# Splitting the dequantised weights on ScalarE and GpSimd instead of GpSimd alone, with another order of TensorE's small steps, in a fused attention and LoRA kernel

## The reference

```python
x + attention(xn) + ffn(xn)
# attention: q, k, v = xn @ ((qw - 8) * repeat(scales, 128)); 32 query heads and 8 key/value heads of 128,
#            rope on q and k, scores / sqrt(128), causal softmax, values, then @ ((qw_o - 8) * scales_o)
# ffn:       xn @ W_base.T + b_base + 2 * sum over the two best of 8 experts of p_e * ((xn @ A_e.T) @ B_e.T)
```

## Time and profile before

| | us |
|---|---|
| runs | 2031.89, 2031.93 |
| the profiled execution | 2028.99 |
| its span | 2027.2 |
| TensorE busy in it | 1987.2 (98%) |
| VectorE, ScalarE, GpSimd busy | 1488.9, 983.2, 1527.7 |

### The profile page before, as it was taken

One profiled execution on the slowest core, in us unless ns is written; L12 is line 12 of the kernel. 1 busy time (PEld: TensorE's weight loads), 2 busy tenths in 40 slices (PEclk: granted clock), 3 DMA queues, 4 the chain that ended last, 5 costly groups with the idle time before them and its releaser, 6 DMA issues.

```text
span 2027.2 us, 31353 instructions
## 1 busy us (share of the span) xinstructions
PE 1987.2 (98%) x10666; PEld 1693.1 (84%) x10668; DVE 1488.9 (73%) x3059; ACT 983.2 (48%) x2202; POOL 1527.7 (75%) x1376
## 2 busy tenths in 40 slices
PE   8999999999999999999989999999999999999998
PEld 6888888888888888888878888888888888888887
DVE  6757777777777777677766777777777777767775
ACT  3145554454544455455534545445554545545453
POOL 2657789677878779786886869867787877968683
PEclk9999999999999999999999999999999999999999
DMA  6326465454635546453583645454464545535454
GB/s 227 137 73 154 110 153 136 127 135 120 167 110 136 130 135 158 110 151 105 151 223 110 208 126 157 116 153 128 118 156 115 146 115 155 158 94 141 126 147 112
DMA packets 302422, 280.17 MB, mean 138 GB/s; under 512 B 34584, under 2 KB 215736, under 8 KB 301752
## 3 DMA queue, kind: packets, MB, share of 16 engines
q1 hardware_dynamic: 298808, 272.13, 50.3%
q0 software_dynamic: 2112, 4.19, 0.7%
q10 hardware_dynamic: 1344, 1.85, 0.3%
HBM read 200.25 MB, written 77.94 MB: 137 GB/s over the span
## 4 chain that ended last, share of the span: by engine, by line
PE 74%; DMA 8%; DVE 7%; POOL 7%; issue 2%; SPq 1%; ACT 1%; DVEq 0%; POOLq 0%; ACTq 0%
PE ring L1317 37%; PE O_ps L1317 16%; PE ring L1451 16%; PE turned L1462 5%; DMA moved<-squares 5%; POOL moved_low L797 3%; DMA squares<-probs 2%; DVE probs L1194 2%; DVE ctx_f L1224 1%; POOL scl L739 1%; DVE probs L1187 1%; SPq L608 1%; POOL W_low L759 1%; POOL ctx_low L821 1%; DVE rope L1171 1%
## 5 line engine op out<-in xcount | busy, mean ns | idle before, releaser
L945 ACT ACTIVATE probs<-probs,negmax 128x128 f32<-128x128 f32 (+7 forms) x512 | 396.2, 774 | 153.5 <-DVE negmax L1187 153.3
L1187 DVE CUSTOM_DVE_ANT_0 probs<-ring,mask_row 128x128 f32<-128x128 f32 (+7 forms) x512 | 373.6, 745 | 41.1 <-PE ring L1451 40.8
L797 POOL TENSOR_TENSOR moved_low<-moved,moved_high 128x512 fp32r<-128x512 f32 x256 | 328.7, 1293 | 76.0 <-ACT moved_high L871 74.6
L1100 DVE TENSOR_TENSOR PT_low<-turned,PT_high 128x512 fp32r<-128x512 f32 (+3 forms) x515 | 245.2, 489 | 178.4 <-ACT PT_high L871 97.2
L871 ACT ACTIVATE PT_high<-turned 128x512 fp32r<-128x512 f32 (+3 forms) x515 | 213.6, 433 | 324.1 <-PE turned L1462 301.5
L821 POOL TENSOR_TENSOR ctx_low<-ctx_f,ctx_high 128x512 fp32r<-128x512 f32 (+1 forms) x131 | 165.9, 1267 | 178.2 <-ACT ctx_high L871 178.2
L804 POOL TENSOR_TENSOR rope<-rope 128x512 f32<-128x512 f32 x160 | 206.9, 1293 | 80.9 <-DVE rope L1172 80.9
L1317 PE MATMUL ring<-xnT_high,W_high 128*128 128x512 f32 x640 | 254.9, 398 | 0.0
L1317 PE MATMUL ring<-xnT_high,W_low 128*128 128x512 f32 x640 | 250.6, 392 | 0.0
L1317 PE MATMUL ring<-xnT_low,W_high 128*128 128x512 f32 x640 | 249.5, 390 | 0.0
L1451 PE MATMUL ring<-K_high,Q_high 128*128 128x512 f32 (+3 forms) x768 | 233.9, 359 | 0.9 <-POOL Q_low L812 0.6
(11 more groups left out here) (124 smaller groups left out, 4680.6 us busy)
## 6 DMA issues: line engine op xcount, KB each, us to landing
squares<-probs SPq DMA_DIRECT2D x256, 256.0 KB, 2.9
moved<-squares SPq DMA_DIRECT2D x256, 256.0 KB, 4.7
R_sb<-row_sums SPq DMA_DIRECT2D x128, 256.0 KB, 3.7
scl<-packed_q SPq DMA_DIRECT2D x64, 256.0 KB, 5.0
raw<-in_qw_q SPq DMA_DIRECT2D x64, 256.0 KB, 5.0
scl<-in_scales_o SPq DMA_DIRECT2D x64, 256.0 KB, 4.7
raw<-in_qw_o SPq DMA_DIRECT2D x64, 256.0 KB, 2.9
scl<-packed_k SPq DMA_DIRECT2D x16, 256.0 KB, 4.2
```

The costliest lines, as they stand in the source:

```text
L797: nc.gpsimd.tensor_tensor(out=low, in0=moved[:, :, j, :], in1=high.bitcast(f32), op=ALU.subtract).then_inc(moved_done, 1)
L945: nc.scalar.activation(probs[:, at], probs[:, at], ACT.Exp, bias=negmax[:, i:i + 1], scale=-1.0, accum_out=sums[:, i:i + 1]).then_inc(exp_ ...
L1100: nc.vector.tensor_tensor(out=dst, in0=src, in1=high.bitcast(f32), op=ALU.subtract).then_inc(pt_low, 1)
L1187: nc.vector.tensor_tensor_reduce(row, ps, hidden_keys, -1.0, -MASKED, ALU.add, ALU.min, negmax[:, i:i + 1]).then_inc(negmax_ready, 1)
```

## The change

`W_high` is made by ScalarE, by the same copy that it uses for the other high parts, with the waits that `split_weight` had; GpSimd waits for it with a semaphore of its own and makes `W_low` alone. ScalarE issues the copies 3.0 planned us behind the point at which GpSimd's conversion of the weight is issued. The seven strings of letters get another order of the same letters; some distances of the plan move: GpSimd takes the `moved_low` tiles 0 and 1 15.6 and 18.2 planned us after the scores' last step rather than 13.9 and 14.5, ScalarE's exponentials 1.6 rather than 2.6 behind the scores, and the weights' scales and integers are loaded 1.0 and 1.2 planned us earlier.

```diff
-LATE = "T S T S T S S V V S V T V S S V S V V V"
-LAST = "T S T V T V V S S T V V S S S S V S V V"
+LATE = "T S T S S S V V S V T V S T S V S V V V"
+LAST = "T T V T V V V S S S V T S S S S V S V V"
...
-            scales_due, raw_due = weights_due(STEPS, -7.0), weights_due(STEPS, -6.0)
+            scales_due, raw_due = weights_due(STEPS, -8.0), weights_due(STEPS, -7.2)
...
             def split_weight(u, w):
                 n, slot = weight_number[u, w], SLOT[w]
...
-                if before:
-                    if seen.new(ring_full, ring_number[before]):
-                        pool.wait_ge(ring_full, ring_number[before])
-                if seen.new(scaled, n + 1):
-                    pool.wait_ge(scaled, n + 1)
-                own(nc.gpsimd.tensor_scalar(W_high[:, slot, :], scl[:, n % 2, :], 0.0, 1.0, ALU.add, ALU.mult))
+                if seen.new(w_high_done, n + 1):
+                    pool.wait_ge(w_high_done, n + 1)
                 nc.gpsimd.tensor_tensor(out=W_low[:, slot, :], in0=scl[:, n % 2, :],
                                         in1=W_high[:, slot, :].bitcast(f32), op=ALU.subtract).then_inc(w_done, 1)
...
-            moved_due = [behind(STEPS, us, "scores") for us in (13.9, 14.5)]
-            multiplied = behind(STEPS, 0.1, "values")
+            moved_due = [behind(STEPS, us, "scores") for us in (15.6, 18.2)]
+            multiplied = behind(STEPS, -0.1, "values")
...
+            def weight_high(u, w):
+                n, slot = weight_number[u, w], SLOT[w]
...
+                if before:
+                    if seen.new(ring_full, ring_number[before]):
+                        act.wait_ge(ring_full, ring_number[before])
+                if seen.new(scaled, n + 1):
+                    act.wait_ge(scaled, n + 1)
+                copy(W_high[:, slot, :], scl[:, n % 2, :]).then_inc(w_high_done, 1)
+
...
-            turned_now, scored = behind(STEPS, -0.3, *TURNED), behind(STEPS, 2.6, "scores")
-            projected, rotated = behind(STEPS, 0.1, "rows_v"), behind(STEPS, 4.0, "project")
+            turned_now, scored = behind(STEPS, -0.3, *TURNED), behind(STEPS, 1.6, "scores")
+            projected, rotated = behind(STEPS, -0.9, "rows_v"), behind(STEPS, 4.0, "project")
...
+            weights = weights_due(STEPS, 3.0)
...
+                for u, w in weights[n]:
+                    weight_high(u, w)
```

More of the change, by code:

```diff
@@ L40 @@
 CONTEXTS = 5
[L46 to L49, removed]
-LATE = "T S T S T S S V V S V T V S S V S V V V"
-LAST = "T S T V T V V S S T V V S S S S V S V V"
-LAST_P = "T S T S V S V T P S P V S V V T V S S V P P V S"
+FIRST = "F T F T O V T T V O O O V V"
+FIRST_P = "F F P O T P O T O T P V P T O V V V"
+EARLY = "O T T F F T V O T V O O V V"
+THIRD = "F F T O F T O T V T O V F O V V"
+LATE = "T S T S S S V V S V T V S T S V S V V V"
+LAST = "T T V T V V V S S S V T S S S S V S V V"
+LAST_P = "S T T S V T P V S P V V S V S T V S S P P V V S"
 VALUES = ([0, 1, 2, 3], [0, 4, 5, 1, 6, 2, 7, 3])
@@ L400, in build_program @@
         moved_done = sem("moved_done")
+        w_high_done = sem("w_high_done")
         scaled = sem("scaled")
@@ L918, in high @@
                 copy(dst, src).then_inc(pt_high, 1)
+            def weight_high(u, w):
+                n, slot = weight_number[u, w], SLOT[w]
+                if w[0] == "o":
+                    before = ("output", u - 1, int(w[1]) // 2, NT - 1) if u else ("lora_b", STARTED[1], NT - 1)
+                elif w[0] == "v":
+                    before = ("rows_v", u - 2, VALUES[1][-1]) if u else None
+                elif w in ("q2", "q3"):
+                    before = ("project", u, "q0" if w == "q2" else "k", 1)
+                else:
+                    before = ("project", u - 1, {"q0": "q2", "k": "q3", "q1": "q1"}[w], 1) if u else None
+                if before:
[4 more added lines that the diff above has]
+                copy(W_high[:, slot, :], scl[:, n % 2, :]).then_inc(w_high_done, 1)
             moved_order = itertools.count()
@@ L971, in context_high @@
                     copy(ctx_high[:, at, cols], ctx_f[:, cols]).then_inc(ctx_high_done, 1)
-            turned_now, scored = behind(STEPS, -0.3, *TURNED), behind(STEPS, 2.6, "scores")
-            projected, rotated = behind(STEPS, 0.1, "rows_v"), behind(STEPS, 4.0, "project")
+            turned_now, scored = behind(STEPS, -0.3, *TURNED), behind(STEPS, 1.6, "scores")
+            projected, rotated = behind(STEPS, -0.9, "rows_v"), behind(STEPS, 4.0, "project")
             moved_due = [behind(STEPS, us, "scores") for us in (15.5, 18.1)]
             multiplied = behind(STEPS, -0.2, "values")
-            divided, low_rank = behind(STEPS, 1.2, "values"), behind(STEPS, -0.6, "lora_a")
+            divided, low_rank = behind(STEPS, 1.2, "values"), behind(STEPS, -0.8, "lora_a")
+            weights = weights_due(STEPS, 3.0)
             linear_weights()
```

## The result

The changed kernel takes 2067.31 us, the median of two runs (2066.33 and 2068.28): 1.0184 times the time before, 95% interval 1.0164 to 1.0205. That is 35.4 us more, 31 above my forecast of 2036 and outside the range. The profiled execution took 2068.28 us, its span is 2066.4.

The account below looks back on a forecast made before the run. TensorE was taken as the bound, with 40.0 us idle. The terms summed to +3.9 us on 2028.99, 2032.9 profiled; the runs' median stood 2.92 above, giving 2035.8, said as 2036 us. Range 2018 to 2056.

Parts of the forecast that it names:

- What bounds the kernel.: Whole kernel: TensorE is busy 1987.2 of 2027.2 us, so at most its 40.0 us of idle time can be gained.
- The wait that the change adds, 8 heads, +6.4: Head 0 of odd units: ScalarE's wait for `scl` delays the second `moved_low` and V1, 0.8 us each (0 to 2.0).
- Head 1, 16 heads, +2.4: Head 1 of all units: T6's high part comes late for V6, 0.15 us each (0 to 1.0).
- The other copies stand where ScalarE is idle ... or where GpSimd is ahead; nothing.: Copies ahead of T2, between the last exponentials and in THIRD, among others: no cost, 0.6 us each at worst.
- TensorE's own order: New strings: 471 groups of transposes for 486, -1.4 us, plus separate terms for waits in LAST, LATE and FIRST_P.
- LAST V0: First V of c = 1 in LAST: wait for VectorE's reading of `O_ps` grows by 0.37 us in 8, +3.0 us.
- V3 of FIRST_P: End of FIRST_P: V3's `PT_low` must wait until V1 is done, 0.25 us in 8, +2.0 us.
- V6 of LAST: LAST: V6 gets a longer distance from T6, so waits for `PT_low` shrink, -1.5 us (0 to -2.5).
- LATE: LATE: last V directly ahead of the half still leaves time to read `O_ps`; no cost, 0.5 us of cover.
- The long wait, -7: Mid-run: moved tiles' DMA goes ahead of the `xnT` loads, saving V0's wait and lost clock, bounds 0 and -8.9 us.
- the third rival: Mid-run: moved tiles still share DMA engines with the loads, so -2 us in place of -7: 2041; chance 0.22.
- rival 2: Every half where the copy stands ahead of T6: ScalarE blocks on `scl`, 64 us of waits: 2091; chance 0.08.

Follow-up runs that it names:

- the grid: Table of medians by strings (before, new), due times (before, new) and where `W_high` is made: GpSimd, ScalarE at 6.6 or ScalarE at 3.0.
- the late copy: Changed kernel with ScalarE's copy 3.6 us later in the plan (6.6 for 3.0) and `W_low` as much later, from unit 1 on: 2046.64 us, 1.0086.
- three old strings and the late copy: Changed kernel with the late copy and with FIRST, FIRST_P and LAST as before: 2087.86 us, 1.0268.
- six strings: Kernel before with six of the seven new strings, FIRST staying as before: 2034.90 us, 1.0017.
- seven with V1 behind an O: Kernel before with the seven new strings, but FIRST ending T T O V O O V V: 2034.14 us, 1.0000.
- the four-string kernel: Kernel before with only EARLY, THIRD, LATE and LAST_P new: 2064.70 us, 1.0164.

## Why the prediction was wrong, point by point

By the grid, taken in this order, the 35.4 us are 10.5 for the strings, 4 for the due times and 21 for the copy. In another order the shares are others (the due times first are 48, the strings then give 34 back), and the 4 us are within what the two intervals leave open. My sum had +3.9.

**"What bounds the kernel."** Right: TensorE's stream is the bound, its floor moved by -0.9 us (I had -1.4), and the loss is waiting, with 4.3 us of clock behind waits. Outside the middle the sum had no term for the clock.

**The wait that the change adds, 8 heads, +6.4.** The right copy and nearly the right size, 6.8 us in S4, but by another way; that the number fits is in part luck. V1, which I had waiting, shows no wait in any of the eight, and none of TensorE's 11 waits for `moved_low` is in them. I followed the second `moved_high` to V1. VectorE, which stood 2.02 us before T5's `PT_low`, reads the scores too, and S4 came before V1. I had not asked what else was queued behind the low part.

**Head 1, 16 heads, +2.4.** 4.8 us in 15, at S7 rather than V6, again by way of VectorE. With the copy late it is gone.

**"The other copies stand where ScalarE is idle ... or where GpSimd is ahead; nothing."** This is the step that failed. 129 copies waited, and that of o3 in LAST stands ahead of T4's high part: 9.4 us at V4, and 2.1 us of half clock at V1 and V5 behind it, all gone when that one copy was moved. That is 1.2 us a unit at V4, twice the 0.6 us that I had given as the worst case. The trace of before does not show it by itself: in LAST of unit 6 `raw` and `scl` stand ahead of `K_low` and the second `moved_low` there, and `scl` ends at 944.29, 2.2 us ahead of T4's high part at 946.48. The changed program's order, with `K_low` and two `moved_low` ahead of `raw`, and the lengths of before would have told it. I worked out the copy in two places of a unit and gave the others zero by a sentence.

The Trainium skill, on the page TensorE: Matmul & The Clock Gate, section Step-by-step: what each phase is for, says that TensorE is the only engine that reorders, and that only its weight loads move ahead. The trace agrees: no ScalarE record passes a copy that waits 4.93 us until 1214.92, though the transposes for the two high parts behind it had ended by 1213.15.

**TensorE's own order.** LAST V0: +3.0 expected, +2.3 measured (`ctx_f` 10.9 to 13.0). V3 of FIRST_P: +2.0 expected, +3.4 measured; 0.5 us of the 0.75 each is `V_low`, which I did not name. V6 of LAST: -1.5 and -2.6. LATE: nothing expected, right for V0, and I missed that V2, V3 and S4 had 7.7 us to give. **FIRST was not in the sum at all**, and it was 8.2 us, the second largest row; it had only a clause in the change, and I did not hold its new place of T1, behind the second projection, against VectorE's rope rows.

**The long wait, -7.** The two did change places: SyncE issued the moved tiles at 1041.63, GpSimd the loads at 1043.28. The first tile still took 8.7 us to 1050.35 (14 before), V0 and V1 waited 2.1 and 0.9, and a clock of 0.83 in that stretch cost 1.7 us, where the earlier trace rows have 3.4. 7.2 became 3.5; with the slow products behind, 9.0 became 5.1, so -3.9 for wait and clock: nearer to the third rival's -2 than to the sum's -7. The Trainium skill's rule that each DMA engine takes packets from its queues in turn (DMA: Bandwidth & Descriptors, Queues, rings and completion order) fits that a head start of 1.65 us did not free the tiles of the load, but no run took the loads away.

**Due times.** The second `moved_low` behind `scl` is what I had praised in rival 2 ("what made it late here ... is now behind `scl`"). With the new strings all the due times cost 4 us, with the old ones 47, of which the three numbers of `moved_low` are 40: it needs the strings' places to fit. I took it as a detail of rival 2, and it was a mechanism of its own.

**The rivals.** The second was the right kind: the wait decides, and slower. Its point ("`scl` ends over 3.5 us behind the first `moved_high`") is met in LAST (1214.88 against 1208.94, 5.9 us) and by little not in head 0, where I looked (1487.18 against 1483.73 in unit 11, 3.45 us). Its chance of 0.08 and its 2091 were both off: I had priced it for every head alike.

**Unit 0 and the start** hold another 9 us (V3 of EARLY 3.6; the low-rank steps, their products and an output 5.5), priced nowhere. V3's wait is there with the strings alone (4.8 us). The low-rank steps' is not: counted in the same way over `lora_a`, `lora_b`, `base` and `turn_hidden`, it is 2.7 us before, 2.3 with the strings alone, 2.4 with W_high on GpSimd, 7.2 in the changed kernel and 5.3 with the late copy. But it is 8.3 with the old strings and W_high on GpSimd, so it does not need a copy on ScalarE; the cause stays open. The half clock of the start lasts 10.2 us in the changed kernel, 6.8 in the kernel before and 20.5 in that last run.

## What to carry to other kernels

When an instruction that can wait goes into an in-order queue, lay out the chain at every one of its places, not at the ones that look typical: 32 of 160 copies carried 18 of 21 us, while 169 us of the same engine's waiting at the others cost TensorE some 5. Follow what stands behind it through the next engine's queue as well, to whatever TensorE needs first. And an order and a table of due times are one design: the strings that cost 10 us with the due times of before saved 34 with the new ones, and 45 with the early copy besides; and single strings had no price of their own.

## What was not expected of the hardware

The clock took a part of what the waits took. By the traces it cost 7.6 us before, 11.9 in the changed kernel, 19.3 with the old strings in it, 40.0 with `scl` earlier and 42.2 with three old strings and the late copy, while the two fastest of the new versions (six strings, and seven with V1 behind an O) lost 1.7. These are single executions, and the clock differs between executions of one kernel.

The load of a weight's integers took 8.5 us from issue to use in the four-string kernel (issued 1862.98, `raw` 1871.46) behind four moved tiles and a scale on SyncE's queue, where the page of that kernel has a median of 5.6 us for this load; GpSimd sat 3.82 of them. That the transfers issued just ahead of it made it late was not tested. A wait for such a load belongs behind the work that is due first.
